# A cross-attention and mixture-of-experts kernel: the shared FFN's second bias moves from GpSimd's adds to TensorE matmuls, and the hand-kept places of the work are set anew

## What is computed

```python
h = tanh(ctx @ Ws + layernorm(x) @ W + b)        # for each token and each of 77 context rows, 256 features
att = softmax(h @ w + mask)                      # over the 77 context rows
txt = att @ ctx
x = x + tanh(txt @ Wcw + bcw) * layernorm(x) + tanh(txt @ Wcb + bcb)
y = layernorm(x)
probs = softmax(y @ gate)                        # 8 experts
scores, token_idx = top_k(probs.T, 512)          # each expert takes its 512 best tokens
routed = scatter_add((gelu(y[token_idx] @ W1 + b1) @ W2 + b2) * scores)
shared = gelu(y @ Ws1 + bs1) @ Ws2 + bs2         # bs2, 256 numbers, is what moves
out = x + routed + shared
```

## Time and profile before

| what | value |
|---|---|
| median of three runs (lowest, highest) | 870.93 us (867.70, 870.99) |
| the profiled execution, its own time | 871.19 us |
| its span, first to last instruction | 869.4 us |
| mean granted clock of PE | 0.986 |
| busy PE, PEld | 802.7, 473.0 us |
| busy DVE, ACT, POOL | 735.8, 741.0, 328.4 us |
| ACT's tanh (L1055) in the chain that ended last | 42% |
| PE in that chain, all lines | 34% |

### The profile page before, as it was taken

The page is one execution under the profiler, slowest core; times in us unless marked ns, Lnnn a source line. Parts: engine busy times, 40 slices in busy tenths (PEclk is TensorE's granted clock), DMA queues, the critical chain, the costliest instruction groups (busy, mean ns, idle before and its releaser), DMA issues.

```text
span 869.4 us, 14023 instructions
## 1 busy us (share of the span) xinstructions
PE 802.7 (92%) x5397; PEld 473.0 (54%) x5416; DVE 735.8 (85%) x1420; ACT 741.0 (85%) x525; POOL 328.4 (38%) x451
## 2 busy tenths in 40 slices
PE   7976888878999999999999999999899999999996
PEld 6321222224534353444435545464677999999986
DVE  4789899999889899999999988998887787777651
ACT  3999999999999999999999999997763666666661
POOL 3100420062707004695001309005603377766646
PEclk9899999999999999999999999999999999999999
DMA  8100000000001000100000000002302455544423
GB/s 264 34 1 0 2 1 1 1 24 26 2 1 49 1 1 25 49 25 1 25 1 2 25 25 26 25 1 82 137 25 85 133 148 146 145 115 123 135 25 43
DMA packets 32657, 42.97 MB, mean 49 GB/s; under 512 B 2379, under 2 KB 29135, under 8 KB 32463
## 3 DMA queue, kind: packets, MB, share of 16 engines
q1 hardware_dynamic: 26335, 33.65, 11.8%
q0 software_dynamic: 6144, 8.39, 5.6%
q10 hardware_dynamic: 112, 0.04, 0.0%
HBM read 29.49 MB, written 12.58 MB: 48 GB/s over the span
## 4 chain that ended last, share of the span: by engine, by line
ACT 47%; PE 34%; DVE 8%; issue 7%; POOL 2%; POOLq 0%; ACTq 0%; DVEq 0%
ACT z L1055 42%; PE bank L972 10%; PE bank L990 9%; DVE z L1455 5%; PE bank L903 5%; PE bank L846 3%; PE bank L891 3%; ACT u L1109 2%; ACT z L1051 2%; PE bank L782 1%; PE bank L772 1%; PE bank L1005 1%; PE bank L946 1%; POOL out_dram L1376 1%; ACT hid L1094 0%
## 5 line engine op out<-in xcount | busy, mean ns | idle before, releaser
L1055 ACT ACTIVATE z<-z 128x4096 f32<-128x4096 f32 (+5 forms) x157 | 535.6, 3481 | 4.6 <-DVE z L1455 4.6
L1455 DVE TENSOR_SCALAR z<-feat,txt_bias 128x1024 f32<-128x1024 f32 (+1 forms) x725 | 437.5, 677 | 23.3 <-PE bank L846 22.7
L846 PE MATMUL bank<-z,window 128*32 128x512 f32 x2464 | 298.0, 607 | 41.7 <-ACT z L1055 38.7
L846 PEld LDWEIGHTS bank<-z,window 128*32 128x32 f32 x2464 | 67.3, 110 | 213.8 <-issue 131.3
L903 PE MATMUL bank<-ws_sb,u 128*128 128x256 f32 x512 | 125.3, 390 | 0.0
L903 PEld LDWEIGHTS bank<-ws_sb,u 128*128 128x128 f32 x512 | 94.8, 192 | 37.2 <-issue 23.7
L891 PE MATMUL bank<-tr,ws_s 128*128 128x512 f32 x384 | 105.6, 414 | 3.1 <-issue 1.8
L1247 POOL TENSOR_TENSOR scale<-wb,x_ry 128x4 f32<-128x4 f32 x7 | 5.1, 732 | 268.0 <-ACT wb L1066 268.0
L972 PE MATMUL bank<-xg_s,w_s 128*128 128x512 f32 x384 | 99.1, 396 | 0.2 <-DVE xg_s L1810 0.2
L1145 ACT ACTIVATE hid<-bank,vec 128x512 f32<-128x512 f32 x64 | 44.2, 690 | 55.5 <-PE bank L972 53.4
L990 PEld LDWEIGHTS bank<-w_s,hid_s 128*128 128x128 f32 x672 | 86.7, 188 | 4.5
(11 more groups left out here) (257 smaller groups left out, 781.7 us busy)
## 6 DMA issues: line engine op xcount, KB each, us to landing
w_raw<-in_L_ffn_W_dram SPq DMA_DIRECT2D x16, 1024.0 KB, 5.4
x_ring<-in_x_dram SPq DMA_DIRECT2D x8, 512.0 KB, 8.6
xn_dram<-xn SPq DMA_DIRECT2D x8, 512.0 KB, 2.9
out_dram<-x_ring SPq DMA_DIRECT2D x8, 512.0 KB, 2.9
u<-in_L_ffn_Ws_dram SPq DMA_DIRECT2D x1, 1024.0 KB, 11.1
ws_sb<-in_L_ffn_Ws_dram SPq DMA_DIRECT2D x1, 1024.0 KB, 13.6
b_rep<-in_L_ffn_b_dram SPq DMA_DIRECT2D x1, 1024.0 KB, 8.6
xg<-xn_dram,idx POOLq DMA_INDIRECT x32, 3.4
```

The source lines that it names most:

```text
L846: ins = e.matmul(sums[v][32 * g:32 * g + 32, :], window[:, c, 31 - at_row:63 - at_row], z[:, n % ZB, at_piece:at_piece + TOK], start=(v, g ...
L1055: e.activation(part, part, ACT.Tanh).then_inc(signal(*step), 1)
L1455: ins = e.tensor_scalar(z[:, n % ZB, i * width:(i + 1) * width], feat_of(units, c), bias_of(units, t, c), None, ALU.add)
```

## The change

biased is gone. Two DMAs put bs2 on partitions 0 and 32 of a zeroed tile (bs2_raw, which lies in eq), once POOL has cleared it: a fourteenth constant, and SP waits for the seventh. split_bs2 (DVE, slot 8) makes of it bs2_s in fp32r, the rounded value in row 0 and what is left over in row 32, and bs2_row, a column with ones at 0 and 32. At the first hidden part of every unit PE begins each of the four down sums with a matmul of bs2_row, broadcast to 128 columns, against bs2_s, ahead of the wait for the gelu, and down adds to it. down_end waits for whole instead of biased. The experts' second bias stays on POOL (bias_rows). Block 7 has seven direct pieces instead of five; block 10 has one instead of block 12. PRE, TAIL, FFN and the fill counts have new numbers, most of them one to three blocks away. END_PLACES, GELUS_LATE and EXPERT_FILL place steps of which none are left at that point.

```diff
 SPLITS = ((8, 20), (0, 20), (0, 20), (0, 10))
-FIRST_DIRECT = (7, 7, 1, 3, 1, 4, 0, 5)
+FIRST_DIRECT = (7, 7, 1, 3, 1, 4, 0, 7)
 AHEAD = 3
-DIRECT = (12,)
+DIRECT = (10,)
 PRE = (
-    (0, 0, 4, 1, 1, 3, 2, 4, 3, 7, 10),
-    (18, 16, 19, 20, 22, 21, 24, 24, 26, 27, 29),
-    (28, 19, 27, 29, 31, 31, 33, 32, 36, 36, 40),
-    (15, 19, 24, 19, 20, 21, 27, 24, 28, 24, 25),
-    (26, 26, 28, 29, 30, 32, 30, 34, 35, 34, 39),
-    (17, 21, 26, 23, 23, 24, 26, 27, 29, 27, 28),
-    (17, 25, 29, 29, 30, 32, 34, 33, 36, 33, 34),
+    (0, 0, 4, 0, 1, 3, 2, 4, 3, 7, 10),
+    (18, 16, 19, 20, 22, 21, 24, 22, 26, 27, 29),
+    (28, 19, 24, 29, 31, 31, 32, 32, 36, 36, 40),
+    (16, 16, 21, 19, 20, 21, 27, 23, 28, 24, 25),
+    (26, 26, 27, 28, 29, 31, 31, 33, 34, 33, 38),
+    (16, 24, 24, 23, 23, 24, 26, 27, 29, 27, 28),
+    (17, 25, 28, 29, 32, 32, 34, 33, 36, 33, 34),
 )
 TAIL = (
-    (4, 3, 5, 5, 8, 8, 9, 12, 11, 18, 15, 16, 17, 17, 34),
-    (0, 2, 6, 6, -3, 7, 7, 7, 7, 14, 8, 10, 15, 19, 34),
-    (0, 0, 1, 1, 3, 3, 3, 6, 4, 22, 6, 10, 11, 10, 18),
-    (0, 1, 2, 3, 7, 9, 11, 12, 11, 28, 18, 17, 19, 21, 20),
-    (-1, 0, 1, 1, 4, 5, 5, 5, -3, 9, -2, 8, 10, 10, 26),
-    (-1, 1, 5, 5, 7, 8, 9, 17, 6, 34, 21, 21, 23, 21, 30),
-    (1, 1, 2, 1, 2, 2, 3, 4, 1, 5, 3, 7, 7, 8, 6),
+    (3, 2, 4, 4, 8, 8, 8, 11, 10, 20, 14, 15, 16, 16, 33),
+    (0, 0, 6, 6, -3, 7, 7, 7, 7, 13, 8, 10, 14, 19, 36),
+    (0, 0, 1, 1, 3, 3, 3, 6, 4, 22, 5, 10, 11, 10, 20),
+    (0, 1, 2, 2, 7, 8, 11, 12, 14, 28, 18, 17, 22, 23, 23),
+    (-1, 0, 1, 1, 4, 5, 5, 5, -4, 9, -2, 8, 10, 10, 29),
+    (-1, 1, 2, 5, 7, 8, 11, 15, 4, 34, 20, 19, 21, 19, 29),
+    (0, 0, 1, 0, 1, 1, 2, 3, 0, 5, 2, 6, 6, 7, 8),
 )
 FFN = (
-    (49, 50, 53, 53, 55, 58, 59, 66),
-    (67, 75, 78, 79, 80, 82, 85, 87),
-    (90, 91, 94, 95, 98, 100, 102, 107),
-    (115, 117, 118, 121, 122, 122, 125, 125),
-    (128, 129, 132, 133, 134, 137, 138, 140),
-    (143, 144, 145, 146, 148, 149, 149, 150),
+    (48, 51, 53, 54, 54, 56, 58, 66),
+    (67, 75, 78, 79, 80, 82, 83, 87),
+    (90, 91, 93, 95, 97, 98, 102, 107),
+    (114, 117, 118, 121, 122, 122, 124, 125),
+    (128, 129, 132, 134, 134, 137, 138, 140),
+    (143, 144, 145, 146, 148, 149, 150, 151),
 )
-TOGETHER, TOGETHER_FROM = 2, 92
+TOGETHER, TOGETHER_FROM = 2, 94
 BUSY = (20, 3, 5, 3)
...
 GELUS_LATE = 1
-END_PLACES = (10, 2)
-ENDS_BEHIND = 6
+END_PLACES = (7, 0)
+ENDS_BEHIND = 9
 FFN_STEPS = ("up", "gelu", "down", "down_end", "store_out", "load_x")
...
 BY_VECTOR = ("down_end", "store_out", "load_x")
-
-TAIL_FILL = (3, 5)
+BS2_ROWS, BS2_LOW = 128, 32
+
+TAIL_FILL = (5, 3)
 GELUS_BEFORE = 1
-TEST_FILL = (4, 5, 5, 4, 7, 5, 5, 6, 4, 2)
-RANK_FILL = (1, 5, 7, 0)
-EXPERT_FILL = (16, 4, 7)
-SECOND_FILL = (12, 0, 0, 4, 2)
-LIST_FILL = (2, 0, 0, 1)
+TEST_FILL = (4, 6, 5, 4, 7, 5, 5, 6, 4, 3)
+RANK_FILL = (0, 4, 8, 0)
+EXPERT_FILL = (17, 8, 5)
+SECOND_FILL = (12, 1, 0, 4, 1)
+LIST_FILL = (1, 1, 0, 1)
 PIECES = (4, 2)
-LAST_END = 0
+LAST_END = 1
...
                 [("y_norm", v), ("store_xn2", v)], [("y_turn", v, c) for c in range(C)],
-                *[[("y_turned", v, c)] for c in range(C)], [*(("whole", v, j) for j in range(J)), ("biased", v)]]
+                *[[("y_turned", v, c)] for c in range(C)], [("whole", v, j) for j in range(J)]]
...
     at_slots(0, (9, 11), [[("split_ws1", c)] for c in range(C)])
+    at_slots(0, (8,), [[("split_bs2",)]])
     for bb in range(1, B):
...
         spans, spans_y = [scan[:, 1, i * 2 * J * E:(i + 1) * 2 * J * E].rearrange("p (s j e) -> p s j e", s=2, j=J) for i in range(2)]
+        bs2_raw = eq[0:BS2_ROWS, :]
         early_units = UNITS - 1
...
         early_total, early_inverse = [eq[:, i * NT:i * NT + early_units * J] for i in range(2)]
-        bs2_rep = sb("bs2_rep", [P, D])
+        bs2_s = sb("bs2_s", [BS2_ROWS, D], F32R)
+        bs2_row = sb("bs2_row", [BS2_ROWS, 1], F32R)
         idx = sb("idx", [P, NL, A], I32)
...
         offset_ready = semaphore("offset_ready")
-        CONSTS, MASK_CLEAR = 13, 7
+        CONSTS, BS2_CLEAR, MASK_CLEAR = 14, 7, 8
         vector_link, pool_link = semaphore("vector_link"), semaphore("pool_link")
...
             e.dma_start(ws2_sb[:], Ws2.rearrange("(m p) d -> p m d", p=P)).then_inc(loaded["ws2"], 16)
-            e.dma_start(bs2_rep[:], bs2.partition_broadcast(P)).then_inc(loaded["bs2"], 16)
+            e.wait_ge(consts, BS2_CLEAR)
+            for first in (0, BS2_LOW):
+                e.dma_start(bs2_raw[first:first + 1, :], bs2.unsqueeze(0)).then_inc(loaded["bs2"], 16)
             for v in range(2, XB):
...
                         e.wait_ge(loaded["ws2"], 16)
+                        e.wait_ge(*done("split_bs2"))
                     if m == 0:
-                        for j in range(first + first % 2, end, 2):
-                            take(DOWN[j // 2])
+                        for j in range(first, end):
+                            dst = take(DOWN[j // 2]) if j % 2 == 0 else banks[DOWN[j // 2]]
+                            e.matmul(dst[:, j % 2 * D:(j % 2 + 1) * D], bs2_row[:].broadcast_to([BS2_ROWS, P]), bs2_s[:],
+                                     start=j % 2 == 0, stop=False, skip_group_check=True)
                     e.wait_ge(*done("gelu", v, m))
...
                         ins = e.matmul(banks[DOWN[j // 2]][:, j % 2 * D:(j % 2 + 1) * D], u[:, m % UR, j * P:(j + 1) * P],
-                                       ws2_sb[:, m, :], start=m == 0 and j % 2 == 0, stop=m == M - 1, skip_group_check=True)
+                                       ws2_sb[:, m, :], start=False, stop=m == M - 1, skip_group_check=True)
                     ins.then_inc(signal(*step), 1)
...
             e.memset(window[:], 0.0).then_inc(consts, 1)
+            e.memset(bs2_raw, 0.0).then_inc(consts, 1)
             e.memset(mask_h[0:1], 0.0)
...
                                     ALU.add).then_inc(signal(*step), 1)
-                elif kind == "biased":
-                    v, = args
-                    e.wait_ge(loaded["bs2"], 16)
-                    for j in range(J):
-                        row_of = x_ring[:, v % XB, j, :]
-                        e.wait_ge(*done("whole", v, j))
-                        ins = e.tensor_tensor(row_of, row_of, bs2_rep[:], ALU.add)
-                    ins.then_inc(signal(*step), 1)
                 elif kind == "earlier":
...
                     e.wait_ge(*done("early_exp"))
+                    e.wait_ge(*done("split_bs2"))
                     link(e.tensor_reduce(early_total, early_lg, AX.X, ALU.add))
...
                     e.wait_ge(*done(*summed[v, half]))
-                    e.wait_ge(*done("biased", v))
+                    e.wait_ge(*done("whole", v, J - 1))
                     xs = x_ring[:, v % XB, 2 * half:2 * half + 2, :].rearrange("p j d -> p (j d)")
...
                                     ALU.subtract).then_inc(signal(*step), 1)
+                elif kind == "split_bs2":
+                    low = slice(BS2_LOW, 2 * BS2_LOW)
+                    e.wait_ge(loaded["bs2"], 32)
+                    e.tensor_tensor(bs2_row[:], ident[0:BS2_ROWS, 0:1], ident[0:BS2_ROWS, BS2_LOW:BS2_LOW + 1], ALU.add)
+                    link(e.tensor_copy(bs2_s[:], bs2_raw))
+                    e.wait_ge(vector_link, linked)
+                    e.tensor_tensor(bs2_s[low, :], bs2_raw[low, :], bs2_s[low, :].bitcast(F32),
+                                    ALU.subtract).then_inc(signal(*step), 1)
                 elif kind == "split_lo":
...
```

## The result

| | before | after |
|---|---|---|
| median of 10 runs each, in one comparison, us | 870.43 (867.7 to 871.17) | 867.48 (866.85 to 868.29) |
| ratio after to before, 95% interval | | 0.9972 (0.9961 to 0.9982) |
| profiled execution, us | 871.19 | 867.57 |
| its span, us | 869.4 | 865.8 |

The kernel became faster: by 3.0 us between the two medians, by 0.28% (about 2.4 us; interval 0.18 to 0.39%) in the ratio, which goes by the means. The forecast was 5.5 us faster; the measured time lies in its range, and within the 0.5% that it called no change.

A forecast was written before the change was run, and what follows sets the result against it. ACT and PE were taken to bound the tanh stage, a serial chain the tests, PE the experts. 2.0 us from tanh and 3.5 from tests gave -5.5 on 871.19, or 865.7, median 865.5 us; 8-in-10 range 862.0 to 871.5.

The forecast's parts named there:

- ACT's waits for the adds: Tanh stage: ACT's five waits for DVE's adds, 4.6 us in all, fall to 0.5 us.
- att_shift: Tanh stage, unit 6: ACT's wait for att_shift stays, about 2.2 us instead of 1.88.
- Tanh stage: Up to about 603 us, tanh blocks with ACT and PE full: taken to end 2.0 us sooner.
- PE must follow: Tanh stage behind 490 us: PE's little idle time lets at most 1.6 of 5.3 us of ACT's waits come back.
- Candidate 0.23, no clock fall: Test 3: DVE's candidate instruction takes 0.23 us instead of 2.63; the slower clock in 630 to 635, 1.7 us, goes.
- Tests' stage: Tests for the experts' thresholds: idle 3.2 and clock 1.7 won, bias 0.94 lost, 0.5 given back: 3.5 us.
- Chain and PE are near balance, and I give back 0.5: Tests up to the gathered rows: the serial chain must come forward too, so 4.0 us is cut to 3.5.
- Experts' stage "as long as before": From about 630 us to the end, PE full: a sign of being right was that its length stays unchanged.
- Rival 1: TensorE takes the tanh stage, which gives nothing; only the tests give 3.5 us: 867.5 us, chance 22%.
- Rival 2: Tests: whole holds the candidate as the bias adds did; idle spot and clock fall stay: 869.3 us, chance 12%.
- Rivals 3 and 4: 3: whole's hold comes one test sooner, PE pays all added work, 875.9 us, 10%. 4: all waits go, 862.5 us, 11%.
- rival 5: Adds are slow for other reasons (whole, y_norm); ACT's four waits partly stay: rival 1's time, chance held in its.

The follow-up runs named there:

- bias_only: Kernel after with the places of before, so only the bias moves to TensorE: 867.17 us, ratio 0.996.
- places_only: Kernel before with the numbers of the new places, the bias still on GpSimd: 869.28 us, ratio 0.9982.
- a_noshift: Kernel after with bs2_row laid in unused room, so that no other tile moves: 866.08 us, ratio 0.9947.
- bo_noshift: bias_only with bs2_row laid in unused room, so that no later tile moves: 866.05 us, ratio 0.9947.
- whole_hit: a_noshift with unit 7's whole on GpSimd held until test 2's counts are done, so test 3's candidate falls on it: 866.62 us, ratio 0.9959.
- late7b: Kernel before with unit 7's bias adds on GpSimd made to wait until the ranks are done: 869.57 us, ratio 0.9986.
- late7: Kernel before with unit 7's bias adds moved in the list of steps; they stayed where they were, so a repeat: 869.89 us, ratio 0.9986.
- b_pad32: Kernel before with an unused tile of 32 bytes, so that all later tiles lie 32 bytes higher: 872.56 us, ratio 1.0019.

## Why the prediction missed by half

Point by point, by its own steps:

- **ACT's waits for the adds: right.** 4.6 to 0.5 was said, 0.2 measured. **att_shift: right**, 2.2 said, 2.41 measured. **y_ry: right**, 0.42 left.
- **Tanh stage: right in kind, a little small.** 2.0 us sooner was said, 3.3 measured at the table load, 3.0 at the turn of rho (606.18 to 603.16), which PE has to reach. "PE must follow" is right in kind: PE is 40.00 of 40 and 40.75 of 41 us busy, and in the kernel after the chain that ended last is PE's from 585 to 602 us. It was mis-sized, at 1.6 us to win behind 490 us. With the old places the stage came forward by only 0.8 us (bias_only), within what repeats differ.
- **The price of the matmul: right** (0.07 to 0.17 us against 0.118). **Candidate 0.23, no clock fall: right.** That the fall is due to the idle spot stays open: places_only keeps the hold (2.46 us), PE idles 1.9 us behind it, and its granted clock in 630 to 635 is 1.00. Its profiled execution (867.93) is one of its faster ones, though (median 869.28):

```profile
630.00:635.00 5.00, 5.00 (x25) 4.06 (x24) 4.34 (x22) 3.17 (x12) 0.00 (x0) 1.00 0.01 2
```

- **Tests' stage: the first term that failed.** 3.5 us was said, 67.78 - 66.46 = 1.3 measured. The 3.5 is what the bias alone gives (64.28 in bias_only). The stage in before, after and bias_only, columns as in rows 1:

```profile
603.11:670.89 67.78, 62.50 (x358) 48.14 (x351) 53.17 (x196) 38.21 (x98) 20.94 (x31) 0.97 0.23 77
```

```profile
599.79:666.25 66.46, 62.77 (x370) 48.05 (x363) 51.12 (x197) 38.24 (x98) 18.78 (x27) 1.00 0.24 81
```

```profile
602.29:666.57 64.28, 61.57 (x366) 47.97 (x359) 50.14 (x196) 38.23 (x98) 18.18 (x26) 1.00 0.23 76
```

  The forecast took 2.7 us from PE's idle time (3.2 less the 0.5 given back) and 0.8 from its busy time (clock 1.7, bias 0.94 the other way). bias_only does this: idle 5.28 to 2.71, busy 62.50 to 61.57. In after the idle time falls by 1.6 only (5.28 to 3.69), and the busy time rises by 0.3. "Chain and PE are near balance, and I give back 0.5" is the step that failed. With the new places the idle time came back as waits of PE for the lists (0.39), for the gathered rows (0.81) and for the first of their split parts (0.34); the prediction had named "PE waiting at the gathered rows" as a sign of being wrong. Of the 1.1 us of busy time too much, 0.7 are sums of the last blocks: PE, full in the tanh stage, does 2.57 us of work between the table load and the turn of rho, where before it did 1.88. So the savings of the two stages were added as if they were independent, and they are not. Why the chain itself is longer with the new places was not found.
- **Experts' stage "as long as before": the second that failed.** It is 1.0 us longer, and no step spoke of it. In the diff it is the line `bs2_row = sb("bs2_row", [BS2_ROWS, 1], F32R)`, which was read as a tile and not as 32 bytes ahead of other tiles. In all it costs 1.4 us in the medians; without it the change gives 870.93 - 866.08 = 4.85 us (a_noshift), within 0.7 of the forecast. Part of that nearness is luck: its tests' stage still gives 1.2 us instead of 3.5, and its tanh stage more than was said.
- **Rivals.** Rival 1 gives nearly the measured time (867.5), but for another reason: its tanh stage did not stand still. Its mechanism may show with the old places (2.3 us of bo_noshift's tanh stage, one execution). Rival 2 needs a hold of 2 us under `whole`, and whole_hit shows 0.3. Rivals 3 and 4 did not come, and rival 5 is refuted: with the adds gone ACT's waits are, too (0.2 us).

Together: adds on GpSimd gone -6.2, matmuls +1.5, shift +1.4, which is -3.3, against -3.0 measured. The first two add up to bo_noshift by the way they were measured, so the sum tests only that the places add nothing and that the shift costs after the same. The held candidate and the clock's fall are in the profiled execution of the kernel before; if they are not in all its runs, a part of the forecast was never in the median. How much of the 0.7 left is that, is open.

## What to carry to other kernels

Of a new tile, however small, ask where it puts the tiles allocated behind it: here 32 bytes cost half of what the change won, and laying them in unused room gave it back. A saving in one stage and one in the next add up only if the same engine bounds both; here TensorE was full at the end of the first stage and near balance with a serial chain in the second, and of 3.3 us won in the first, 2.2 were missing from the second, half as idle time of TensorE and half as work that it still had to do. And before a stall in a profile is priced, look at the spread of the runs: one execution shows it at one size.

## What was not expected of the hardware

- Tiles shifted by 32 bytes of each partition: groups of twelve matmuls at 1.43 instead of 1.41 us, the experts' stage 189.87 to 189.89 us in three kernels, against 188.8 to 188.9 in those shifted by 0 or 64 (one of them, whole_hit, is at 189.25).
- A DVE instruction of 0.23 us takes 2.46 to 2.63 beside GpSimd's TENSOR_TENSOR and 0.52 beside its TENSOR_SCALAR of the same 128x256. DVE instructions with one tensor input are slowed beside the former too: in late7b slot_a takes 0.82 us instead of 0.29.
- The clock's fall behind an idle spot of 2.1 us stands in three executions, before, late7 and b_pad32 (0.66 to 0.68), and did not come behind one of 1.9 us in the one of places_only.
